# Reordering one unit of the first cross-attention on TensorE

## The reference

```python
def _mha_cross(x, mem, in_w, in_b, out_w, out_b):
    B, L, D = x.shape
    H = NHEAD                      # 16
    hd = D // H                    # 8
    ...
    q = _split_heads(x @ wq.T + bq, H)
    k = _split_heads(mem @ wk.T + bk, H)
    v = _split_heads(mem @ wv.T + bv, H)
    scores = jnp.einsum('bhqd,bhkd->bhqk', q, k) * (1.0 / math.sqrt(hd))
    attn = jax.nn.softmax(scores, axis=-1)
    out = _merge_heads(jnp.einsum('bhqk,bhkd->bhqd', attn, v))
    return out @ out_w.T + out_b
```

## Time and profile before

| | us |
|---|---|
| median of 3 runs | 3433.33 (3430.18 to 3441.29) |
| the profiled execution, its own time | 3437.91 |
| its span, first to last instruction | 3436.0 |
| TensorE busy, share of the span | 3282.3, 96% |
| VectorE busy, share of the span | 2386.2, 69% |
| mean granted TensorE clock, share of full speed | 0.973 |

### The profile page before, as it was taken

One profiled execution on the slowest core, in us unless ns is written; L12 is line 12 of the kernel. 1 busy time (PEld: TensorE's weight loads), 2 busy tenths in 40 slices (PEclk: granted clock), 3 DMA queues, 4 the chain that ended last, 5 costly groups with the idle time before them and its releaser, 6 DMA issues. The chain is left out here.

```text
span 3436.0 us, 67280 instructions
## 1 busy us (share of the span) xinstructions
PE 3282.3 (96%) x26181; PEld 1891.3 (55%) x26320; DVE 2386.2 (69%) x5439; ACT 1907.4 (56%) x2599; POOL 1612.3 (47%) x1271
## 2 busy tenths in 40 slices
PE   6899999999997898999999999999999998989999
PEld 4566666666655674555545555455544544655555
DVE  8778778778774536777777777777777775653333
ACT  6466666666664234666666666666666663432222
POOL 5433343333322104777777777777777764300000
PEclk8699999999999899999999999999999999989999
DMA  2133333333310002101111011110111101000000
GB/s 75 38 73 78 82 74 75 77 78 77 76 41 1 26 1 74 39 21 38 39 39 39 20 39 39 39 39 20 39 39 39 33 17 50 1 28 4 4 4 4
DMA packets 90541, 138.92 MB, mean 40 GB/s; under 512 B 14512, under 2 KB 67824, under 8 KB 89456
## 3 DMA queue, kind: packets, MB, share of 16 engines
q1 hardware_dynamic: 90224, 134.61, 14.5%
HBM read 94.15 MB, written 1.05 MB: 28 GB/s over the span
## 5 line engine op out<-in xcount | busy, mean ns | idle before, releaser
L2490 ACT ACTIVATE arena<-banks,arena 128x512 f32<-128x512 f32 x832 | 560.3, 687 | 476.6 <-PE banks L2279 476.6
L2304 PE MATMUL banks<-arena 128*128 128x512 f32 x1664 | 803.9, 603 | 0.8 <-ACT arena L2497 0.8
L2238 POOL TENSOR_TENSOR arena<-arena 128x1024 f32<-128x1024 f32 x256 | 603.8, 2359 | 165.7 <-ACT arena L2497 164.6
L1250 DVE TENSOR_REDUCE arena<-banks 128x1 f32<-128x512 f32 (+1 forms) x896 | 529.1, 627 | 162.5 <-PE banks L1084 157.9
L2392 DVE TENSOR_TENSOR banks<-arena,banks 128x512 f32<-128x512 f32 x640 | 444.3, 694 | 241.9 <-ACT arena L2490 221.1
L1390 ACT ACTIVATE arena<-banks 128x1024 f32<-128x1024 f32 (+1 forms) x448 | 423.7, 961 | 277.3 <-PE banks L1164 277.1
L2409 DVE TENSOR_TENSOR arena<-arena,banks 128x1024 f32<-128x1024 f32 (+1 forms) x448 | 507.2, 1133 | 1.6 <-PE banks L2294 1.2
L2497 ACT ACTIVATE arena<-arena 128x1024 f32<-128x1024 f32 (+1 forms) x448 | 443.0, 989 | 11.1 <-DVE arena L2409 10.9
L2304 PEld LDWEIGHTS banks<-arena 128*128 128x128 f32 x1664 | 289.9, 190 | 220.8 <-issue 200.3
L2279 PE MATMUL banks<-arena 128*128 128x512 bf16 x830 | 313.2, 377 | 2.5
L2278 PE MATMUL banks<-arena 128*128 128x512 bf16 x786 | 297.9, 379 | 4.1
(11 more groups left out here) (356 smaller groups left out, 5116.7 us busy)
## 6 DMA issues: line engine op xcount, KB each, us to landing
arena<-arena SPq DMA_DIRECT2D x768, 50.0 KB, 2.2
arena<-in_ctxT SPq DMA_DIRECT2D x32, 800.5 KB, 6.3
arena<-in_ctx SPq DMA_DIRECT2D x32, 768.0 KB
fold<-in_ctxT SPq DMA_DIRECT2D x16, 800.5 KB, 4.6
foldv<-in_ctxT SPq DMA_DIRECT2D x16, 800.5 KB, 4.7
arena<-in_m2w SPq DMA_DIRECT2D x3, 2048.0 KB, 8.0
arena<-in_xw SPq DMA_DIRECT2D x1, 2048.0 KB, 8.0
weights<-in_weights SPq DMA_DIRECT2D x1, 1920.0 KB, 11.5
```

The lines of the kernel that those rows point to most:

```text
L1250: eng.tensor_reduce(o, s, AX, ALU.max).then_inc(a_max, 1)
L2238: eng.tensor_tensor(part, part, tiles, ALU.add).then_inc(sums, 1)
L2304: eng.matmul(c.ps[:, R_MIX + v % 2, :], ctxn[:, b, kt * D:(kt + 1) * D], st[:, v % 2, kt, :], start=kt == 0, stop=kt == KT - 1).then_inc(m ...
L2490: eng.activation(st[:, v % 2, kt, :], c.ps[:, n % SB, :], ACT.Identity, bias=hide[:, kt, v // 2:v // 2 + 1])\
```

## The change

Of a unit, the same matmuls of maxima, scores, mixes, values, keys and queries are kept and put in another order, in which neighbours of one array shape stand together: mixes in twos, queries beside a chunk of keys, blocks of maxima next to scores. The chunks of values and keys are taken in the order 0, 3, 1, 2 (`PARTS`), so that the small one (65 keys) is the second. Final, queries and that small chunk lie in different columns of bank 7 (`FAT`, `QAT`) and may be in it together (`share_bank7`); whoever takes the bank next waits for all of them. Before DVE reads the final it waits for ACT to have copied the small chunk. The shifts add the queries on TensorE by two more matmuls in each unit, and DVE only copies the sum. The orders of DVE and ACT are written to match.

```diff
-    chunks = [(0, 512), (512, 1024), (1024, 1536), (1536, S)]
+    PARTS = (0, 3, 1, 2)
+    chunks = [(512 * p, min(512 * p + 512, S)) for p in PARTS]
+    QAT, FAT = P, P + 4 * L
...
-    held = {"until": None}
+    held = {"until": []}
 
     def take_bank7(eng, until):
 
-        if held["until"] is not None:
-            eng.wait_ge(*held["until"])
-        held["until"] = until
+        for freed in held["until"]:
+            eng.wait_ge(*freed)
+        held["until"] = [until]
+
+    def share_bank7(eng, until):
+        held["until"].append(until)
...
-        for kt in range(4 * n, min(4 * n + 4, KT)):
+        for kt in range(4 * PARTS[n], min(4 * PARTS[n] + 4, KT)):
...
-    def pe_query(eng, i, b, bank):
+    def pe_query(eng, i, b, bank, at=0):
         for s in range(4):
-            mm = eng.matmul(c.ps[:, bank, s * L:(s + 1) * L], c.W("c_wq", s * P, (s + 1) * P),
+            mm = eng.matmul(c.ps[:, bank, at + s * L:at + (s + 1) * L], c.W("c_wq", s * P, (s + 1) * P),
                             c.xT[:, i, b * L:(b + 1) * L], start=True, stop=True)
...
-        def keys(i, b, n):
-            take_bank7(eng, (k_copied, i * 8 + 4 * b + n + 1))
+        def keys(i, b, n, bank7=take_bank7):
+            bank7(eng, (k_copied, i * 8 + 4 * b + n + 1))
             pe_key(eng, i, b, n, 7)
 
-        def values(i, b, n):
-            take_bank7(eng, (v_made, i * 8 + 4 * b + n + 1))
+        def values(i, b, n, bank7=take_bank7):
+            bank7(eng, (v_made, i * 8 + 4 * b + n + 1))
             pe_value(eng, i, b, n, 7)
 
         def queries(i, b):
-            take_bank7(eng, (q_made, i * 2 + b + 1))
-            pe_query(eng, i, b, 7)
+            share_bank7(eng, (q_made, i * 2 + b + 1))
+            pe_query(eng, i, b, 7, QAT)
...
-                mm = eng.matmul(o, lt[:, s2, :], unit, start=True, stop=True)
+                eng.matmul(o, lt[:, s2, :], unit, start=True, stop=False)
+                mm = eng.matmul(o, unit, q4a[:, v // 2, 2 * (v % 2) + s2, :], start=False, stop=True)
...
-            for at, a, b in ((0, "num_a", "num_b"), (L, "den_a", "den_b")):
+            for at, a, b in ((FAT, "num_a", "num_b"), (FAT + L, "den_a", "den_b")):
...
-                for st in range(STEPS):
-                    if st == STEPS - 1:
-                        mix(i, v, st)
-                    if st < 5:
+                old = i + v > 0
+
+                def other(n, bank7=take_bank7):
+                    if v % 2 == 0:
+                        if here(2):
+                            values(*((i, 1) if v == 0 else (i + 1, 0)), n, bank7)
+                    elif more:
+                        keys(i + 1, v // 2, n, bank7)
+
+                def highest(a):
+                    if a < STEPS:
                         if here(1):
-                            maxima(*later(i, v, 1), st + 2)
+                            maxima(*later(i, v, 1), a)
                     elif here(2):
-                        maxima(*later(i, v, 2), st - 5)
-                    if st < 4:
-                        n = st
-                        if v % 2 == 0:
-                            if here(2):
-                                values(*((i, 1) if v == 0 else (i + 1, 0)), n)
-                        elif more:
-                            keys(i + 1, v // 2, n)
-                    elif st == 4:
-                        if i + v > 0:
-                            final(*later(i, v, -1))
-                    elif st == 6 and v % 2 == 1 and more:
+                        maxima(*later(i, v, 2), a - STEPS)
+
+                highest(2)
+                other(0)
+                scores(i, v, 2)
+                highest(3)
+                if old:
+                    final(*later(i, v, -1))
+                    if v % 2 == 1 and more:
                         queries(i + 1, v // 2)
-                    if st < STEPS - 1:
-                        mix(i, v, st)
-                    if st < 5:
-                        scores(i, v, st + 2)
-                    if st == 5 and here(1):
-                        shifts(*later(i, v, 1))
+                other(1, share_bank7 if old else take_bank7)
+                mix(i, v, 0)
+                mix(i, v, 1)
+                scores(i, v, 3)
+                highest(4)
+                other(2)
+                scores(i, v, 4)
+                highest(5)
+                other(3)
+                mix(i, v, 2)
+                mix(i, v, 3)
+                scores(i, v, 5)
+                highest(6)
+                scores(i, v, 6)
+                highest(7)
+                mix(i, v, 4)
+                mix(i, v, 5)
+                if here(1):
+                    shifts(*later(i, v, 1))
+                mix(i, v, 6)
+                highest(8)
...
-            if v % 2 == 0:
-                eng.wait_ge(q_spread, i * 4 + v + 2)
-            eng.tensor_tensor(q4b[:, v % 2], c.ps[:, 7, 0:2 * P].rearrange("p (s q) -> p s q", q=P),
-                              q4a[:, v // 2, 2 * (v % 2):2 * (v % 2) + 2, :], ALU.add).then_inc(q4b_made, 1)
+            eng.tensor_copy(q4b[:, v % 2].rearrange("p s q -> p (s q)"), c.ps[:, 7, 0:2 * P]).then_inc(q4b_made, 1)
...
-            eng.reciprocal(rd[r, :], c.ps[r, 7, L:2 * L]).then_inc(f_rec, 1)
+            eng.reciprocal(rd[r, :], c.ps[r, 7, FAT + L:FAT + 2 * L]).then_inc(f_rec, 1)
             eng.wait_ge(f_rec, n + 1)
-            eng.tensor_tensor(c.o[r, i, b * L:(b + 1) * L], c.ps[r, 7, 0:L], rd[r, :], ALU.mult).then_inc(f_out, 1)
+            eng.tensor_tensor(c.o[r, i, b * L:(b + 1) * L], c.ps[r, 7, FAT:FAT + L], rd[r, :], ALU.mult).then_inc(f_out, 1)
 
...
-                for st in range(STEPS):
-                    if st == 0 and old:
-                        mask_mix(*later(i, v, -1))
-                    if st < 5:
+
+                def highest(a):
+                    if a < STEPS:
                         if here(1):
-                            maxima(*later(i, v, 1), st + 2)
+                            maxima(*later(i, v, 1), a)
                     elif here(2):
-                        maxima(*later(i, v, 2), st - 5)
-                    if st == 4 and here(1):
-                        spread_max(*later(i, v, 1))
-                    if st == 4 and old:
-                        final(*later(i, v, -1))
-                    if st == 5 and here(1):
-                        add_shift(*later(i, v, 1))
-                    if st == 6 and v % 2 == 1 and more:
+                        maxima(*later(i, v, 2), a - STEPS)
+
+                if old:
+                    mask_mix(*later(i, v, -1))
+                highest(2)
+                highest(3)
+                if old:
+                    if v % 2 == 0:
+                        if here(2):
+                            eng.wait_ge(v_made, i * 8 + (6 if v == 0 else 10))
+                    elif more:
+                        eng.wait_ge(k_copied, (i + 1) * 8 + 4 * (v // 2) + 2)
+                    final(*later(i, v, -1))
+                    if v % 2 == 1 and more:
                         queries(i + 1, v // 2)
+                for a in range(4, STEPS):
+                    highest(a)
+                if here(1):
+                    spread_max(*later(i, v, 1))
+                highest(7)
+                if here(1):
+                    add_shift(*later(i, v, 1))
+                highest(8)
...
-                for st in range(STEPS):
-                    exps(i, v, st)
-                    if 1 <= st < 5:
-                        n = st - 1
-                        if v % 2 == 0:
-                            if here(2):
-                                values(*((i, 1) if v == 0 else (i + 1, 0)), n)
-                        elif more:
-                            keys(i + 1, v // 2, n)
+
+                def other(n):
+                    if v % 2 == 0:
+                        if here(2):
+                            values(*((i, 1) if v == 0 else (i + 1, 0)), n)
+                    elif more:
+                        keys(i + 1, v // 2, n)
+
+                exps(i, v, 0)
+                other(0)
+                exps(i, v, 1)
+                other(1)
+                exps(i, v, 2)
+                exps(i, v, 3)
+                other(2)
+                exps(i, v, 4)
+                other(3)
+                exps(i, v, 5)
+                exps(i, v, 6)
...
```

More of the change, by code:

```diff
@@ L1231, in pe, with dve_query @@
         final(PAIRS - 1, UNITS - 1)
-    def dve_query(eng, i, b, bank):
+    def dve_query(eng, i, b, bank, at=0):
         eng.wait_ge(q_ps, i * 2 + b + 1)
         wait_if(eng, q_spread, i * 4 + 2 * b)
-        eng.tensor_tensor(qf, c.ps[:, bank, 0:4 * L].rearrange("p (s q) -> p s q", q=L), spread(c.W("c_bq"), L),
+        eng.tensor_tensor(qf, c.ps[:, bank, at:at + 4 * L].rearrange("p (s q) -> p s q", q=L), spread(c.W("c_bq"), L),
                           ALU.add).then_inc(q_made, 1)
@@ L1276, in queries @@
         def queries(i, b):
-            dve_query(eng, i, b, 7)
```

(8 more changed lines are left out.)

## The result

The changed kernel takes 3524.9 us (median of 4 runs, 3518.6 to 3528.2) against 3433.4 for the one before in the same comparison: 1.0254 times as long, 95% interval 1.0238 to 1.0271, or 91 us more. The forecast was 3479, with a range to 3503. The direction was right; half of the loss had not been seen.

A forecast was written before the change was run, and what follows sets the result against it. TensorE's issue and its waits for DVE were taken as the bound. Per two units, -1.04 issue, -2.13 old waits and +4.7 new ones gave +1.5 us; times 30, +45 us: about 3479, eight in ten 3455 to 3503.

The forecast's parts named there:

- The three priced waits: Three places per unit where TensorE lacks work to cover DVE's maxima: 2.05 us per unit, 4.10 in two.
- the saved changes: TensorE's issue: 10 fewer changes of array shape in two units save 1.28 us, net 1.04 after the shifts' extra matmuls.
- the fixed exchange: Last block of a unit to next unit's first: 1.75 us to the second half's start, 0.66 covered, wait 1.09.
- the block behind it: Block of maxima after a unit's first block, a chunk of values and 8 scores: a wait of 0.31 us.
- the large block behind the small one: Small block, last scores, next large block: 0.89 us needed against 0.24 of work, a wait of 0.65.
- the fourth chunk of keys: Bank 7, with only 8 scores and a block after the third chunk: a wait of 0.30 us.
- the third: Third chunk of keys waits for DVE's adding of queries behind the division: between 0 and 0.4 us, taken as 0.1.
- the waits that go: TensorE's waits for DVE at the ends of units in the kernel before, all taken off: 2.13 us in two units.
- the one that priced the parts' new order: POOL splits a full chunk last and ends later; with later chunks this takes some 2.5 of the keys' DMAs' 3 us.
- That the waits would stay as they are: Rival: the order saves 1.04 us in two units, 31 in all, waits unchanged, time 3402; chance 0.08.
- that the two cancel: Rival: new waits near 3.2 us instead of 4.7 in two units, time 3425 to 3443; chance 0.06.
- The rival that was slower through the keys: Rival: POOL ends later, keys' DMAs come 1 us late in each of 31 spans, time 3510; chance 0.06.

The follow-up runs named there:

- the kernels without the collision: The changed kernel with POOL's work in the stage cut to one column per instruction (3481.7 us), or with POOL's last chunk of keys held until DVE's shift (3480.4 us).
- the run with short maxima: The kernel before, with the large blocks' maxima reading 64 columns instead of 512: 3375.7 us, ratio 0.9821; the changed kernel with the same cut: 3433.8 us.
- the last kernel: The kernel before, parts unchanged, in an order keeping 1.75 us of other work between starts of neighbouring blocks of maxima wherever it can: 3409.9 us, ratio 0.9906.
- the kernel with the late split: The changed kernel, all work kept, POOL starting the last chunk of keys only when DVE has made the shift: 3480.4 us, ratio 1.0122.
- the kernel with the filled wait: The changed kernel with three useless matmuls of 512 columns ahead of the shifts' wait in odd units: 3508.2 us, ratio 1.0204.

## Why the prediction was half right

**The three priced waits and the saved changes: right.** In the changed kernel's rows the fixed exchange is 1.77 (forecast 1.75), the block behind it waits 0.28 (0.31), the large block behind the small one comes 0.63 after the last scores began instead of 0.12 and takes 0.43 instead of 0.31, together 0.63 (0.65), the fourth chunk of keys 0.31 (0.30), and the third some 0.1 for the division (0.1). The sum of all is tested by the kernels without the collision: +1.33 in two units, against +1.5. Of the waits that go, 2.13, the run with short maxima bears out 27.22 - 25.31 = 1.91. A change of shape costs what I took: two mixes together take 452.53 - 451.51 = 1.02, two apart 2 x 0.57, the difference is 0.12.

**The step that failed is the one that priced the parts' new order.** The prediction said: "The small chunk was the last to be split, now a full one is, so POOL ends later", and followed POOL's lateness to one place only, the DMAs of the keys, which had 3 us to spare and still have enough (no wait for them shows on TensorE). What else runs beside POOL in those 2.2 us was not asked. It is DVE's shift, 0.17 and 0.23 us of work with TensorE's shifts right behind it. The trace of before had only a faint warning, since its last split is short: two of the 64 L1289 took 0.28 and 0.29, both begun 0.04 after the start of POOL's subtraction of 65 columns (L1011), and both in the spans in which the clock had fallen. Cost: 0.87 (29.42 - 28.55) in each of 30 spans, 26 us.

The Trainium skill has the rule that I did not weigh, in "SBUF — State Buffer", section "Who interferes with whom": a DVE instruction with two SBUF inputs contends with a GpSimd instruction that reads SBUF. The same section of the Trainium skill calls the port pair that the two share an exclusive lock, and says that the order of issue decides who blocks. The rows agree: both held instructions have two SBUF inputs and begin inside a POOL instruction, and each ends 0.02 to 0.09 us after it; L1290 in the kernel with `PARTS` alone, begun 0.02 before POOL's, isn't held. The maxima from PSUM are never held, nor is the TENSOR_REDUCE of 128x16 from SBUF. Casts with one SBUF input can be, as the last kernel shows; in the changed kernel none of the 30 began inside a POOL instruction that outlasted it.

**The second failed step is a term that was left out: the clock.** The sum took every duration at full rate, since the earlier trace rows had 0.99 for the stage. Waits were priced as time lost and no more. With two fixed waits, the shifts' wait and bank 7's in a short stretch, the granted clock fell to the 1.2 GHz level 17 times in the stage, at 1.2 us each; filling the shifts' wait gave back 17 us of the median and 21 of the profiled stage.

**The sum that the runs give**, by the stage from first to last of these rows: 899.7 - 857.0 = 42.7 us for the priced part (the kernel with the late split; forecast 45), 923.1 - 899.7 = 23.4 for the hold-up (from there to the kernel with the filled wait), and 944.1 - 923.1 = 21.0 for the clock. The 23.4 are below the 26 given above because the kernel with the late split has two falls of the clock of its own at the end of the stage, at 1.2 us each. The second and third go together: the late split takes both away, up to these two.

**The rivals.** That the waits would stay as they are (3402) is refuted by the exchange's 1.77; that the two cancel (near 3435), which needed the small block and bank 7 to cost almost nothing, by the 0.63 and 0.31 there and by the 1.33 without the collision. The rival that was slower through the keys had the right edit and the wrong road: POOL does end later, and it is DVE that pays, not the transfers. How near it was is seen in the late split, where TensorE waited for the transfers, if only for 0.2 and 0.35 us. The sign stands on the priced waits alone, since without the collision the kernel is still 1.2% slower.

**What stays open.** Why the lower clock came in some spans and not in every one, and the exact part of the wait in it, no run isolates; nor what the held CAST costs the last kernel.

## What to carry to other kernels

A change of array shape cost about a tenth of a microsecond here, and a block of maxima 1.75 from its start to the bank's reuse: order the work so that each reuse has that much of other work ahead of it, and save changes of shape only where that leaves the cover whole. When an edit moves the work of an engine for which the bottleneck never waits, look at what now runs beside it, not only at who takes its result: a four-element instruction of DVE took six times as long beside a POOL instruction. A wait that comes back in each round is to be priced at the clock it may cost too; matmuls with no use in it are a cheap test.

## What the runs showed of the hardware

- DVE's TENSOR_TENSOR of 128x4 from two SBUF operands took 0.17 us, and up to 1.07 when a POOL instruction on SBUF was under way at its start; its end follows POOL's end by some 0.02 us. Begun 0.02 before the POOL instruction (`PARTS` alone), the same took 0.17.
- A CAST of 128x4 with one SBUF input took 0.77 to 0.79 us instead of 0.17 in the last kernel, begun inside POOL's 128x512. The TENSOR_REDUCE in front of it, begun inside the same POOL instruction, kept its 0.17.
- A kernel with throw-away matmuls in a wait was 17 us faster than the same one without. With DVE's maxima short, the same wait at the shifts, 30 times 0.83, brought no fall of the clock.
- Taking one wait away let another grow: with DVE's maxima short, the four waits for ACT's copies out of bank 7 went from 41.7 to 63.3 us.
